# A wait on the eleventh evicted count step ahead of GpSimd's edge-list gathers in a graph layer

## The chip, the cores and the metric

The kernel runs on one core of one Trainium2 chip. The metric is the device time of one execution, in microseconds (us). Before the change three runs took 560.68, 562.6 and 565.33 us; their median is 562.6 us.

## What is computed

```python
msg = node_feat[src] + edge_feat
agg = jax.ops.segment_sum(msg, dst, num_segments=node_feat.shape[0])
h = jax.nn.relu(agg @ W1 + b1)
return h @ W2 + b2
...
h = jnp.maximum(_layernorm(x, axis=-1), 0.0)
x = x + _L0_gnn_ref(h, edge_attr_64, src, dst, ...)
```

There are 6250 nodes with 64 features and 206250 edges, each with a source node, a destination node and 64 features of its own. The edges are sorted by destination, and each node has its own loop among them. All values are float32 and all indices are int32. For every node the kernel adds up the normalized rows of the sources of its edges and the features of the edges, puts the sum through a layer of 128 hidden units, and adds the result to the node's row.

## The kernel before, in words

**Tiles and periods.** The nodes are cut into 49 tiles of 128, and two tiles are taken at a time. So there are 25 periods, j = 0 to 24; LAST = 24 is the short one, with one tile. In a period TensorE does three kinds of work. It counts, for the nodes of period j, how many edges come from each of the 6250 source nodes. It multiplies the counts of the period before, m = j - 1, with the rows of h. And it puts the pair of tiles f = j - 2 through the hidden layer.

**Counting.** A node has at most 64 edges in its list. GpSimd gathers the lists of the two tiles with two indirect DMAs (`gather_slots`, L490 to L500, into `ell`). VectorE marks the slots that belong to the node (`match`, L633 to L645, writing `hi_m`). TensorE turns the list (`turn_codes`, L778 to L785), ScalarE copies it as `codes` (L354). VectorE makes one-hot matrices of its low and high parts, `lo_hot` and `hi_hot` (`hots`, L647 to L663), in four batches of 32 nodes a period. TensorE multiplies them, 16 small matmuls in a count step (`count`, L799 to L813), and there are 16 count steps in a period. Step u fills a buffer of PSUM, and ScalarE evicts it to `counts` (`copy_counts`, L383 to L389). Each eviction adds one to the semaphore `copied`.

**TensorE's order.** Its order within a period is written out in eight parts, v = 0 to 7 (L871 to L915). Each part begins with count steps 2v and 2v + 1. Then come 12 or 13 matmuls with 256 columns: L823, the high sums, in the even parts, and L831, the low sums, in the odd ones. The odd parts go on with matmuls of 24 float32 columns, L845, the edge sums. Part 0 also has the hidden layer, L860, and part 1 its second matmul, L867. Part 3 turns the edges' destinations, L795, and part 4 turns the lists of the next period, L784 and L785.

**VectorE's order.** Each batch of `hots` waits for its codes and for the count step that freed its buffer (L651 to L653). The first batch of period j + 1 so waits for count step 11 of period j, and the second for step 15. After batch 0 and batch 1 comes an edge one-hot, L670; after batch 1 `match(j + 1)` and `add_rows(j - 2)`, L682; after batch 2 `count_below(j + 2)`, L609 and L616; after batch 3 `set_pointers(j + 2)`, L630, which writes `rp_f`, the place in the sorted edges at which the list of each node begins.

**GpSimd's order.** Its loop over j is at L522 to L532. It issues the two row gathers for period j + 1 (`gather_rows`, L469, into `g`), waits for `rp_f` of period j, places the ranges (`place_ranges`, L479, L481 and L485), issues the two list gathers (L496), then makes the edges' relative destinations of period j - 1 (`make_rel`, L507) and adds the bias to rows of x (`add_bias`, L515). GpSimd runs about two periods ahead of TensorE: the lists of period j are gathered while TensorE counts period j - 2. SyncE's queue loads the edge features, two DMAs for each tile, when the buffer of a tile four back has been used.

Of the kernel before, what the change touches and what calls it, by code (L numbers as in the profile page):

```python
# [6 lines left out]
def build_gnn_layer(nc, x, src, dst, edge, w1, b1, w2, b2, out):  # L7
# [14 lines left out]
    LAST = NT // 2  # L22
# [24 lines left out]
    def step_index(j, u):  # L47
        return 16 * j + u
# [25 lines left out]
    with ctx:  # L74
# [6 lines left out]
        def sem(name):  # L81
            return ctx.enter_context(nc.semaphore(name))
# [131 lines left out]
        hots_made, counted, copied = sem("hots_made"), sem("counted"), sem("copied")  # L214
# [13 lines left out]
        with nc.Block() as block:  # L228
# [11 lines left out]
            def _(sp):  # L240
# [44 lines left out]
                for j in range(DTS):  # L285
                    if j < LAST:
                        sp.wait_ge(r0_made, j + 1)
                        _, firsts = nc.values_load_multi_w_load_instructions(
                            r0_i[0:1, 2 * j:2 * j + 2], engines=[mybir.EngineType.SP], min_val=0, max_val=E - RANGE,
                            skip_runtime_bounds_check_because="held to the last range of edges")  # L290
                    else:
                        firsts = [E - RANGE]
                    if j >= 2:
                        sp.wait_ge(rel_made, j - 1)
                    for h in range(tiles_in(j)):
                        load_dst_rows(j, h, firsts[h])
                    if j == 0:
                        load_weights()
                        sp.wait_ge(matched, 1)
                    for h in range(tiles_in(j)):  # L300
                        load_edges(2 * j + h, firsts[h])
                    if j == 2:
                        with nc.allow_non_contiguous_dma(reason="the first dst of each following row"):
                            sp.dma_start(dst_sb[0:ROWP - 1, PER:PER + 1],
                                         dst[PER:E].rearrange("(p e) -> p e", e=PER)[:, 0:1]).then_inc(next_in, 16)
                        sp.dma_start(dst_sb[ROWP - 1:ROWP, PER:PER + 1],
                                     dst[E - 1:E].rearrange("(p e) -> p e", e=1)).then_inc(next_in, 16)
                        sp.wait_ge(h_made, SLICES)
                        sp.dma_start(h_dram.rearrange("(t p) f -> p t f", p=P), h_sb[:, :, :]).then_inc(h_out, 16)
                    if j >= 2:  # L310
                        store_rows(j - 2)
# [106 lines left out]
            def _(pool):  # L418
# [45 lines left out]
                def gather_rows(j):  # L464
                    if j >= 2:
                        pool.wait_ge(below_made, j - 1)
                    for h in range(tiles_in(j)):
                        t = 2 * j + h
                        nc.gpsimd.indirect_dma_start(  # L469
                            out=g2[j % 2][:, h, :], out_offset=None, in_=dst.rearrange("(r e) -> r e", e=STEP),  # L470
                            in_offset=bass.IndirectOffsetOnAxis(ap=row_i[:, t:t + 1], axis=0)).then_inc(rows_in[j % 2], 16)

                def place_ranges(j):
                    n = tiles_in(j)
                    if j >= 2:
                        pool.wait_ge(ell_in[j % 2], 32 * (j // 2))
                    pool.wait_ge(rp_made, j + 1)
                    if j < LAST:
                        nc.gpsimd.tensor_scalar(r0_f[0:1, 2 * j:2 * j + n], rp_f[0:1, 2 * j:2 * j + n],  # L479
                                                float(E - RANGE), None, ALU.min).then_inc(r0_set, 1)  # L480
                    nc.gpsimd.tensor_scalar(ell_idx[j % 2][:, 0:n], rp_f[:, 2 * j:2 * j + n],  # L481
                                            float(E), None, ALU.min).then_inc(idx_made, 1)
                    if j < LAST:
                        pool.wait_ge(r0_set, j + 1)
                        nc.gpsimd.tensor_copy(r0_i[0:1, 2 * j:2 * j + n], r0_f[0:1, 2 * j:2 * j + n]).then_inc(r0_made, 1)  # L485
                    else:
                        pool.wait_ge(shift_made, 1)
                        nc.gpsimd.tensor_copy(ell_idx[j % 2][0:HALF, 1:2], shift_f[0:HALF, :]).then_inc(idx_made, 1)

                def gather_slots(j):  # L490
                    pool.wait_ge(idx_made, j + 1 + (j == LAST))
                    if j >= 2:
                        pool.wait_ge(turned, j - 1)
                    for h in range(2):
                        rows = HALF if j == LAST and h == 1 else P
                        nc.gpsimd.indirect_dma_start(  # L496
                            out=ell[j % 2][0:rows, h, :, :].rearrange("p s w -> p (s w)"), out_offset=None,
                            in_=comb_dram[:, :],
                            in_offset=bass.IndirectOffsetOnAxis(ap=ell_idx[j % 2][0:rows, h:h + 1], axis=0)
                        ).then_inc(ell_in[j % 2], 16)  # L500

                def make_rel(j):
                    n = tiles_in(j)
                    pool.wait_ge(dst_rows_in[j % 2], 32 * (j // 2) + 16 * n)
                    if j >= 2:
                        pool.wait_ge(rel_turned, j - 1)
                    nc.gpsimd.tensor_scalar(rel_rows[j % 2][0:n * CK, :], dst_rows[j % 2][0:n * CK, :],  # L507
                                            float(2 * j * P), tile_base[0:n * CK, 0:1],
                                            ALU.subtract, ALU.subtract).then_inc(rel_made, 1)

                def add_bias(f):
                    tiles = slice(2 * f, 2 * f + tiles_in(f))
                    pool.wait_ge(mean_sub, SLICES)
                    pool.wait_ge(w_in, 80)
                    nc.gpsimd.tensor_tensor(x_sb[:, tiles, :], x_sb[:, tiles, :],  # L515
                                            bc(b2_all[:, :].rearrange("p (o f) -> p o f", o=1), [P, tiles_in(f), F]),
                                            ALU.add).then_inc(bias_added, 1)
# [4 lines left out]
                for j in range(DTS):  # L522
                    if j + 1 < DTS:
                        gather_rows(j + 1)
                    place_ranges(j)
                    if j == 0:
                        pool.wait_ge(comb_out, 48)
                    gather_slots(j)
                    if j >= 1:
                        make_rel(j - 1)  # L530
                    if j >= 2:
                        add_bias(j - 2)  # L532
# [542 lines left out]
```

## Time and profile before

| | |
|---|---|
| median of three runs | 562.6 us (560.68 to 565.33) |
| profiled execution | 561.41 us, span 559.8 us |
| TensorE matmul (PE) | 486.8 us busy, 87% of the span |
| VectorE (DVE) | 428.1 us, 76% |
| ScalarE (ACT) | 355.1 us, 63% |
| GpSimd (POOL) | 268.7 us, 48% |
| mean granted clock of TensorE | 0.988 |

The profile is of one execution; its span is from the first to the last instruction. PE are matmuls, PEld weight loads, which run beside them. A row of the timeline gives the start in us from the beginning of the span, the time in us, the engine, the line of the kernel, the operation with what it writes and reads, and how many instructions are merged in the row. Where the engine sat idle before, the row ends with that idle time and what ended it. "issue" stands for idle time in which the engine waited for nothing that the profile shows.

### The profile page before, as it was taken

The page shows a single profiled execution, that of the slowest core. Times are in us where ns is not written, and L with a number is a line of the kernel's source. Part 1 is how long each engine was busy: PE and PEld are TensorE (multiplying, and loading weights), DVE is VectorE, ACT ScalarE, POOL GpSimd, SP SyncE. Part 2 cuts the span into 40 slices and gives each one's busy share as a digit, 9 for nine tenths or more (in the row PEclk, how much of TensorE's full clock was granted, in tenths as well). Part 3 has the DMA queues.
Part 4 walks back from the last instruction along what each step waited for, and adds up shares of the span by engine and source line. Part 5 has one row for each costly group of instructions (what it writes and reads, how often), then busy time and mean ns, then how long its engine had stood idle before and what let it go on. Part 6 is the DMA issues. An engine that isn't in the chain of part 4 may idle for free.

```text
span 559.8 us, 27476 instructions
## 1 busy us (share of the span) xinstructions
PE 486.8 (87%) x12541; PEld 427.6 (76%) x12541; DVE 428.1 (76%) x456; ACT 355.1 (63%) x503; POOL 268.7 (48%) x249
## 2 busy tenths in 40 slices
PE   1014999999999999999999999999999999998996
PEld 1013788777888888888888888888888888887895
DVE  4999879667887797777787787777788779766941
ACT  3747667665766767656666666666676676575721
POOL 4483774484375366336357347417437535416200
PEclk9999999998999999989999999999999999899999
DMA  9575167453453543633634635435546354354300
GB/s 201 162 216 165 24 200 193 127 167 105 112 176 102 154 141 100 188 102 97 189 105 117 174 101 150 140 99 151 141 110 180 100 154 138 97 152 123 94 7 9
DMA packets 139623, 73.62 MB, mean 132 GB/s; under 512 B 23644, under 2 KB 137550, under 8 KB 139382
## 3 DMA queue, kind: packets, MB, share of 16 engines
q1 hardware_dynamic: 136105, 65.30, 42.4%
q0 software_dynamic: 3168, 4.90, 2.7%
q8 instruction: 99, 1.62, 1.2%
q10 hardware_dynamic: 234, 1.65, 0.9%
q14 instruction: 17, 0.14, 0.1%
HBM read 66.98 MB, written 4.86 MB: 128 GB/s over the span
## 4 chain that ended last, share of the span: by engine, by line
PE 84%; DVE 8%; issue 5%; ACT 1%; DMA 1%; another core or an unknown queue 0%; SPq 0%; DVEq 0%; ACTq 0%
PE sum_ps L823 25%; PE sum_ps L845 20%; PE count_ps L810 18%; PE sum_ps L831 14%; PE head_ps L860 3%; PE head_ps L867 3%; DVE lo_hot L656 2%; PE turn_ps L795 1%; DVE hi_hot L656 1%; DMA dst_sb<-in_dst 1%; DVE h_sb L555 1%; DVE mean L553 1%; DVE h_sb L568 1%; DVE var L561 1%; DVE h_parts L624 1%
## 5 line engine op out<-in xcount | busy, mean ns | idle before, releaser
L387 ACT CAST counts<-count_ps 128x784 bf16<-128x784 f32 x391 | 300.9, 817 | 129.0 <-PE count_ps L810 124.6
L656 DVE TENSOR_TENSOR lo_hot<-iota_lo,codes 128x4096 bf16<-128x4096 bf16 x98 | 224.1, 2286 | 66.8 <-PE count_ps L810 54.4
L823 PE MATMUL sum_ps<-counts,h_parts 128*128 128x256 bf16 (+1 forms) x1225 | 153.8, 277 | 0.0
L845 PE MATMUL sum_ps<-e_hot,edges 128*64 128x24 f32 x3528 | 129.6, 215 | 15.8 <-issue 15.6
L810 PE MATMUL count_ps<-hi_hot,lo_hot 64*128 64x49 bf16 x6256 | 124.9, 184 | 19.1 <-DVE hi_hot L656 11.5
L845 PEld LDWEIGHTS sum_ps<-e_hot,edges 128*64 128x64 f32 x3528 | 124.9, 138 | 20.5 <-issue 19.3
L810 PEld LDWEIGHTS count_ps<-hi_hot,lo_hot 64*128 64x128 bf16 x6256 | 101.5, 95 | 42.8 <-issue 13.4
L823 PEld LDWEIGHTS sum_ps<-counts,h_parts 128*128 128x128 bf16 x1225 | 114.1, 100 | 20.2 <-issue 0.2
L479 POOL TENSOR_SCALAR r_f<-rp_f 1x2 f32<-1x2 f32 x24 | 12.8, 533 | 188.9 <-DVE rp_f L630 188.8
L469 POOL DMA_INDIRECT g<-in_dst,row_i x49 | 88.0, 1796 | 18.3 <-issue 11.5
L656 DVE TENSOR_TENSOR hi_hot<-iota_hi,codes 128x1600 bf16<-128x1600 bf16 x98 | 96.5, 985 | 0.0
L831 PE MATMUL sum_ps<-counts,h_parts 128*64 128x256 bf16 (+1 forms) x1225 | 86.2, 275 | 0.0
L507 POOL TENSOR_SCALAR rel_rows<-dst_rows,tile_base 36x256 f32<-36x256 int32 (+1 forms) x25 | 71.6, 2864 | 4.4 <-DMA dst_rows<-in_dst 2.5
L496 POOL DMA_INDIRECT ell<-comb_rows,ell_idx x50 | 60.4, 1208 | 22.1 <-issue 17.0
L831 PEld LDWEIGHTS sum_ps<-counts,h_parts 128*64 128x64 bf16 x1225 | 59.7, 110 | 5.2 <-issue 0.2
L670 DVE TENSOR_TENSOR e_hot<-win_tab,rel_sb 128x864 f32<-128x864 f32 x49 | 54.8, 1118 | 6.1 <-ACT rel_sb L363 6.1
L372 ACT COPY agg_sb<-sum_ps 128x256 f32<-128x256 f32 (+1 forms) x25 | 9.2, 367 | 27.3 <-issue 11.9
L642 DVE SCALAR_TENSOR_TENSOR hi_m<-ell,node_f 128x64 bf16<-128x64 f32 x50 | 11.9, 278 | 17.4 <-DMA ell<-comb_rows,ell_idx 13.3
L784 PE MATMUL turn_ps<-ident_b,ell 128*128 128x128 bf16 x25 | 5.6, 223 | 21.4 <-DVE hi_m L642 19.0
L682 DVE TENSOR_TENSOR o_sb<-head_ps,x_sb 128x128 f32<-128x128 f32 (+1 forms) x25 | 7.1, 286 | 18.4 <-PE head_ps L867 18.4
L354 ACT COPY codes<-turn_ps 128x512 bf16<-128x512 bf16 x25 | 14.7, 587 | 9.9 <-PE turn_ps L785 9.9
L784 PEld LDWEIGHTS turn_ps<-ident_b,ell 128*128 128x128 bf16 x25 | 2.8, 112 | 21.9 <-issue 21.7
(108 smaller groups left out, 222.3 us busy)
## 6 DMA issues: line engine op xcount, KB each, us to landing
edges<-in_edge_attr SPq DMA_DIRECT2D x98, 576.0 KB
h_rows<-h_sb SPq DMA_DIRECT2D x1, 1568.0 KB, 10.1
x_sb<-in_x SPq DMA_DIRECT2D x4, 384.0 KB, 10.5
out<-o_sb SPq DMA_DIRECT2D x24, 64.0 KB, 3.7
comb_rows<-counts ACTq DMA_DIRECT2D x1, 1443.8 KB
dst_rows<-in_dst SPq DMA_DIRECT2D x49, 18.0 KB
ell<-comb_rows,ell_idx POOLq DMA_INDIRECT x50
g<-in_dst,row_i POOLq DMA_INDIRECT x49
```

What stands on the lines that cost most here:

```text
L387: nc.scalar.copy(counts[j % 2][:, :, 0:2 * half].rearrange("p s (h i) -> p h s i", h=2)[:, :, :, 8 * u:8 * u + 8], count_ps[g % 2][:, :, 0 ...
L469: nc.gpsimd.indirect_dma_start(out=g2[j % 2][:, h, :], out_offset=None, in_=dst.rearrange("(r e) -> r e", e=STEP), in_offset=bass.Indirect ...
L496: nc.gpsimd.indirect_dma_start(out=ell[j % 2][0:rows, h, :, :].rearrange("p s w -> p (s w)"), out_offset=None, in_=comb_dram[:, :], in_off ...
L507: nc.gpsimd.tensor_scalar(rel_rows[j % 2][0:n * CK, :], dst_rows[j % 2][0:n * CK, :], float(2 * j * P), tile_base[0:n * CK, 0:1], ALU.subt ...
L656: return nc.vector.tensor_tensor(out_ap.rearrange("p i (a t) -> p i a t", t=2), bc(table_ap.rearrange("p (o a t) -> p o a t", o=1, t=2), [ ...
L670: nc.vector.tensor_tensor(e_hot[h][:, :, :].rearrange("p (c k) w -> p c k w", k=KK), bc(win_tab[:, m // LAST, :, :].rearrange("p c (o w) - ...
L810: last = nc.tensor.matmul(count_ps[g % 2][:, h, i * NT:(i + 1) * NT], lo_hot[n % 2][rows, at, :], hi_hot[n % 2][rows, at, 0:NT], start=Tru ...
L823: nc.tensor.matmul(sum_ps[m % 2][:, 0:cols], parts[:, s, 0:2 * F], counts[m % 2][:, s, 0:cols], start=(s == 0), stop=False, skip_group_che ...
L831: last = nc.tensor.matmul(sum_ps[m % 2][half, 0:cols], parts[:, s, 2 * F:3 * F], counts[m % 2][:, s, 0:cols], start=False, stop=False, ski ...
L845: last = nc.tensor.matmul(sum_ps[m % 2][half, low:low + W], edges[t % SLOT_EDGES][:, c, k * F:(k + 1) * F], e_hot[h][:, i, :], start=False ...
L860: nc.tensor.matmul(hid_ps[:, 0:cols], w1_sb[:, :], agg_sb[:, 0:cols], start=True, stop=True).then_inc(hid_made, 1)
L867: last = nc.tensor.matmul(out_ps[0:n, h * F:(h + 1) * F], hid_sb[:, h * P:h * P + n], w2_sb[:, :], start=True, stop=True)
```

## The change

GpSimd gets one more wait, behind `place_ranges(j)` and ahead of `gather_slots(j)`, in the loops with j from 2 to 24. It waits until ScalarE has evicted count step 10, the eleventh, of period j - 2. For every j that occurs the expression gives step 10, since j - 2 is below LAST. Nothing else is changed.

```diff
                     place_ranges(j)
                     if j == 0:
                         pool.wait_ge(comb_out, 48)
+                    if 2 <= j:
+                        pool.wait_ge(copied, step_index(j - 2, 10 if j - 2 < LAST else 0) + 1)
                     gather_slots(j)
                     if j >= 1:
                         make_rel(j - 1)
```

## Rows read from the trace of the kernel before

**Rows 1.** The chain of waits that ended last, its shares by engine
```profile
PE 84%; DVE 8%; issue 5%; ACT 1%; DMA 1%; another core or an unknown queue 0%; SPq 0%; DVEq 0%; ACTq 0%
```

**Rows 2.** Waits: who waited for whom, us in total, times, longest
```profile
PE sum_ps L845 <- issue: 15.6, 39, 0.4
...
DVE hi_m L642 <- DMA ell<-comb_rows,ell_idx: 13.3, 4, 4.7
```

**Rows 3.** Timeline of GpSimd over one period
```profile
296.27 0.22 POOL L479 TENSOR_SCALAR r_f<-rp_f 1x2 f32<-1x2 f32 x1 [8.43 <-DVE rp_f L630]
...
297.25 1.00 POOL L496 DMA_INDIRECT ell<-comb_rows,ell_idx  x1 [0.47 <-issue]
298.56 0.94 POOL L496 DMA_INDIRECT ell<-comb_rows,ell_idx  x1 [0.30 <-issue]
299.59 3.19 POOL L507 TENSOR_SCALAR rel_rows<-dst_rows,tile_base 36x256 f32<-36x256 int32 x1
...
303.48 2.91 POOL L469 DMA_INDIRECT g<-in_dst,row_i  x1 [0.16 <-issue]
306.69 1.48 POOL L469 DMA_INDIRECT g<-in_dst,row_i  x1 [0.30 <-issue]
```

**Rows 4.** Timeline of TensorE, the same period and the next one's start
```profile
296.75 0.58 PE L810 MATMUL count_ps<-hi_hot,lo_hot 64*128 64x49 bf16 x32
...
299.30 0.31 PE L845 MATMUL sum_ps<-e_hot,edges 128*64 128x24 f32 x4 [0.40 <-issue]
300.01 0.48 PE L845 MATMUL sum_ps<-e_hot,edges 128*64 128x24 f32 x10 [0.40 <-issue]
...
305.46 0.70 PE L860 MATMUL head_ps<-agg_sb,w_sb 128*128 128x256 f32 x2
...
325.60 0.70 PE L860 MATMUL head_ps<-agg_sb,w_sb 128*128 128x256 f32 x2
```

**Rows 5.** Timeline of VectorE over the same period
```profile
295.95 0.15 DVE L630 TENSOR_TENSOR rp_f<-cnt,row_base 128x2 f32<-128x2 f32 x1
298.64 2.29 DVE L656 TENSOR_TENSOR lo_hot<-iota_lo,codes 128x4096 bf16<-128x4096 bf16 x1 [2.54 <-PE count_ps L810]
...
305.39 0.98 DVE L656 TENSOR_TENSOR hi_hot<-iota_hi,codes 128x1600 bf16<-128x1600 bf16 x1
...
307.26 0.47 DVE L642 SCALAR_TENSOR_TENSOR hi_m<-ell,node_f 128x64 bf16<-128x64 f32 x2
```

**Rows 6.** Timeline of ScalarE, the same stretch
```profile
296.85 0.58 ACT L354 COPY codes<-turn_ps 128x512 bf16<-128x512 bf16 x1 [0.20 <-PE turn_ps L785]
297.34 0.82 ACT L387 CAST counts<-count_ps 128x784 bf16<-128x784 f32 x1
298.57 0.81 ACT L387 CAST counts<-count_ps 128x784 bf16<-128x784 f32 x1 [0.42 <-PE count_ps L810]
```

**Rows 7.** Timeline of GpSimd in an early period
```profile
92.37 2.12 POOL L479 TENSOR_SCALAR r_f<-rp_f 1x2 f32<-1x2 f32 x1 [7.43 <-DVE rp_f L630]
...
96.47 3.04 POOL L496 DMA_INDIRECT ell<-comb_rows,ell_idx  x1 [0.16 <-issue]
99.82 1.51 POOL L496 DMA_INDIRECT ell<-comb_rows,ell_idx  x1 [0.30 <-issue]
```

**Rows 8.** Timeline of VectorE in the same early period
```profile
104.96 0.48 DVE L642 SCALAR_TENSOR_TENSOR hi_m<-ell,node_f 128x64 bf16<-128x64 f32 x2 [4.45 <-DMA ell<-comb_rows,ell_idx]
```

**Rows 9.** Timeline of TensorE, the starts of three early periods
```profile
77.72 0.67 PE L860 MATMUL head_ps<-agg_sb,w_sb 128*128 128x256 f32 x2
...
98.13 0.70 PE L860 MATMUL head_ps<-agg_sb,w_sb 128*128 128x256 f32 x2
...
119.08 0.70 PE L860 MATMUL head_ps<-agg_sb,w_sb 128*128 128x256 f32 x2 [0.27 <-ACT agg_sb L372]
```

**Rows 10.** Timeline of GpSimd, a row gather of 1 us
```profile
242.20 0.96 POOL L469 DMA_INDIRECT g<-in_dst,row_i  x1 [0.30 <-issue]
```

**Rows 11.** Timeline of TensorE behind two such pairs of row gathers
```profile
125.37 0.47 PE L810 MATMUL count_ps<-hi_hot,lo_hot 64*128 64x49 bf16 x22 [0.48 <-issue]
...
243.58 0.89 PE L845 MATMUL sum_ps<-e_hot,edges 128*64 128x24 f32 x23 [0.37 <-issue]
```

## The prediction

> **What bounds the kernel now.** I read the chain of waits first: TensorE holds 84% of it, and "issue" another 5% [rows 1]. So only time in which TensorE stands still counts, and VectorE (76% busy) and GpSimd (48%) matter through what they do to it. The table of waits then says where TensorE stands still without a producer being late: 15.6 us ahead of the edge sums L845, in 39 pieces of at most 0.4 us [rows 2]. The timelines of one period, side by side, show where they lie. GpSimd issues its two list gathers at 297.25 and 298.56, 1.00 and 0.94 us long [rows 3]; TensorE pauses for 0.40 us up to 299.30 and again for 0.40 us up to 300.01, both in the edge sums of part 5 [rows 4]. The same pair stands at the same distance behind the gathers, 1.6 us and 2.4 us after the start of the first, in each of the 18 periods from 133.68 to 480.50. The other three pieces follow row gathers. Those are 36 pieces in 18 periods, 14.7 us of the 15.6 (0.37, 0.33 and 0.21 us are the other three).
>
> The gathers do more than that. Count steps 10 and 11 start at 296.75 and end at 297.33 [rows 4], and the codes are there at 296.85 + 0.58 = 297.43 [rows 6]. Yet ScalarE gets step 11 only at 298.57, after 0.42 us of idleness [rows 6], and VectorE starts the next batch at 298.64, after 2.54 us [rows 5]. Both come 0.3 to 0.4 us after the end of the first gather, 298.25. I take it that a gather holds up TensorE's signals and its supply of instructions for about its last microsecond. The long matmuls L823 and L831 hide such a hold, and a run of short ones, L845 or the count steps, does not. The row gathers of the same period speak for this: they end at 306.39 and 308.17, among L823 and L867, and leave no gap.
>
> **The change, step by step.**
> One: when the wait opens. Step 10 is evicted at 297.34 + 0.82 = 298.16 [rows 6]. With the 0.3 us that GpSimd takes between gathers [rows 3] the first list gather starts at 298.45 in place of 297.25, 1.2 us later. In the first periods the gather is already later than the eviction (96.47, period start 98.13 [rows 7, 9]), and the wait costs nothing.
>
> Two: what the gather then meets. With no gather running, the signal of step 11 comes at once, so VectorE starts `lo_hot` at about 297.55 and ends `hi_hot` 3.19 us later (the same pair is 3.19 from 298.64 on), at 300.74. The first gather falls into it. In the row gathers [rows 3] one that starts beside `lo_hot` takes 2.91 us and ends at 306.39, with `hi_hot`, whose end is 305.39 + 0.98 = 306.37 [rows 5]; the early list gather takes 3.04 us [rows 7]. So the first list gather ends at 300.75, the second runs from 301.05 for 1.5 us [rows 3, 7] to 302.55, 3.05 us later than the present 299.50. On the lock the Trainium skill ("SBUF — State Buffer", "Who interferes with whom") says that a `tensor_tensor` has no 2-port mode and keeps GpSimd only from reading, and infers that it does not stall descriptor generation. By that rule the first gather would not be stretched; the 2.91 us here disagree.
>
> Three: the pauses of TensorE. The gathers' last microseconds now lie at 299.7 to 300.75 and 301.5 to 302.55. Without its pauses TensorE reaches part 6 at about 299.6: first the short count steps, then the high sums for 1.6 us up to some 301.7, then count steps 14 and 15 and the low sums. The first hold lies in long matmuls, the second mostly behind them, much like the row gathers that leave no gap. I take both pauses as gone: 18 periods, -14.7 us. The bounds are 0 (they only move) and -14.7.
>
> Four: what slides behind. GpSimd's queue behind the wait holds the second list gather, L507, L515 and the next two row gathers. VectorE needs the lists at 307.26, or 306.5 with a period shorter by 0.8. In the early period they landed 104.96 - 101.33 = 3.6 us after the second gather's end [rows 7, 8]; 302.55 + 3.6 = 306.2 is still in time, though by only 0.3 us. L507 is read by TensorE a period later, in part 3, and the biased rows later still; SyncE's load of destinations, which waits for L507, has several microseconds. Nothing is paid there. L507 takes 1.2 us, or stands behind the next batch of hots as now (3.19 us [rows 3]); it ends between 303.8 and 306.1. The row gathers then start between 304.4 and 306.7, and the second ends between 306.7 and 309.1. Against a TensorE that is 0.8 us ahead that is 0.7 us earlier to 1.7 us later than the 308.17 of now. They meet less of the hots and become short, and a pause comes back in the edge sums of part 1: 0.37 us behind a short pair [rows 10, 11]. I take it in every period, 18 x 0.37 = +6.7 us; its bounds are 0 and two of 0.48 us in count steps [rows 11], +17.3 us. ScalarE's eviction of steps 13 and 15 may be held too, which is at most 0.2 us a period in the way of step 0; I take 0, since TensorE's even parts have it covered.
>
> The sum, against the profiled execution: 561.4 - 14.7 + 6.7 = 553.4 us. That execution lies 1.2 us under the median, so about 554.5; I say 554.
>
> **The rivals.**
> A, the forecast: pauses gone in part 5, one comes back in part 1. Range 550 to 558. Chance 0.36.
>
> B, nothing comes back, the row gathers staying behind the hots or hidden in L823: 561.4 - 14.7 = 546.7. For it: now they leave no gap. Chance 0.18.
>
> C, the pauses only change their place. Should the gathers not be stretched, they end at 299.45 and 300.7, and the pauses fall into count steps 12 and 13 at 0.48 us each: 561.4 - 14.7 + 17.3 = 564.0. The same time comes out if the row gathers move into the count steps of part 2. This is what the rule cited under Two would give. Against it stands the stretching to `hi_hot`'s end in 303.48 and 96.47 [rows 3, 7]. Here I count too that the wait is mostly open already. Chance 0.22.
>
> D, slower: the pointers come too late. Now `rp_f` is written by 296.10 [rows 5] and GpSimd's L479 runs at 296.27 in 0.22 us [rows 3], before the next `lo_hot`. VectorE is now free to start that at 297.55, so from 1.3 us of delay in `rp_f` on, L479 stands behind it, as in the early period (2.12 us [rows 7]); L481 and L485 do too, the list gathers slide by some 3 us more, the lists land late (VectorE idle for 4.45 us [rows 8]) and so do the next pointers. What can cause it is the second row gather, up to 1.7 us later against TensorE, holding the signal for L682, behind which batches 2 and 3 stand. The periods in that pattern take 98.13 - 77.72 = 20.41 and 119.08 - 98.13 = 20.95 us [rows 9], against 325.60 - 305.46 = 20.14 [rows 4]: +0.54 on the mean, 18 of them +9.7 us, 571 us. For it: the margin is thin. Against it: the early pattern dissolved by itself after a few periods, so a part of the periods is likelier than all. Chance 0.24.
>
> **How the numbers follow.** The likeliest is A, so 554 us. The range goes from B's 546.5 up to 569, near D's end; outside lie D in full and a few mishaps. About 1% (5.6 us) can be told from no change. Faster by more than that: B, nine tenths of A, a little of D's mixed form: 0.51. Within 1%: the rest of A, C nearly whole, a quarter of D: 0.26. Slower: 0.23.
>
> **What would show it.** Step one: a list gather starts 0.3 us after the eviction of step 10. Step two: VectorE's idle ahead of the first batch's `lo_hot` falls from 2.54 to some 1.4 us, and the first gather takes 2.3 us. Step three: the 39 issue pauses of L845 lose 36, the period falls from 20.14 towards 19.4. Step four: new pauses of 0.4 us behind 1 us row gathers; no DMA wait of L642 beyond the early four [rows 2]. D would show as L479 rows of 2.12 us and more idle of L642 before its lists. I am wrong if the gathers start no later than now, or if the pauses do not depend on where the gathers lie.

## The result and the profile after

The changed kernel takes 544.59 us (median of four runs, 542.93 to 546.33), the kernel before 562.28 us (four runs). The ratio is 0.968, interval 0.9625 to 0.9734: 3.2% faster. Ratios and their intervals, here and below, leave out executions more than 1.5% above the fastest of their kernel; medians and ranges keep them. I had said 554 us and a range from 546.5 us. The profiled execution after takes 545.67 us, its span is 543.8 us.

The waits of all engines after, that answer to [rows 2]:

```profile
POOL ell L496 <- ACT counts L387: 29.8, 18, 2.1
...
DVE hi_m L644 <- DMA ell<-comb_rows,ell_idx: 17.6, 5, 4.7
...
PE sum_ps L847 <- issue: 4.8, 11, 0.4
```

The new wait holds GpSimd 18 times, for 1.7 us each on the mean. (Two lines were added, so the edge sums are L847 now and the list match L644.) TensorE's pauses in the edge sums fell from 15.6 us in 39 pieces to 4.8 us in 11. One period of GpSimd, VectorE and TensorE after, to be laid beside [rows 3], [rows 5] and [rows 4]:

```profile
281.33 1.04 POOL L469 DMA_INDIRECT g<-in_dst,row_i  x1 [0.16 <-issue]
282.68 0.96 POOL L469 DMA_INDIRECT g<-in_dst,row_i  x1 [0.31 <-issue]
...
292.76 2.21 POOL L496 DMA_INDIRECT ell<-comb_rows,ell_idx  x1 [1.65 <-ACT counts L387]
295.27 1.51 POOL L496 DMA_INDIRECT ell<-comb_rows,ell_idx  x1 [0.30 <-issue]
296.87 3.39 POOL L507 TENSOR_SCALAR rel_rows<-dst_rows,tile_base 36x256 f32<-36x256 int32 x1
```

```profile
291.80 2.29 DVE L658 TENSOR_TENSOR lo_hot<-iota_lo,codes 128x4096 bf16<-128x4096 bf16 x1 [1.36 <-ACT codes L354]
294.01 0.98 DVE L658 TENSOR_TENSOR hi_hot<-iota_hi,codes 128x1600 bf16<-128x1600 bf16 x1
```

```profile
278.80 0.70 PE L862 MATMUL head_ps<-agg_sb,w_sb 128*128 128x256 f32 x2
...
282.52 1.19 PE L847 MATMUL sum_ps<-e_hot,edges 128*64 128x24 f32 x27
284.15 0.47 PE L847 MATMUL sum_ps<-e_hot,edges 128*64 128x24 f32 x9 [0.44 <-issue]
284.55 0.58 PE L812 MATMUL count_ps<-hi_hot,lo_hot 64*128 64x49 bf16 x32
...
292.27 1.18 PE L847 MATMUL sum_ps<-e_hot,edges 128*64 128x24 f32 x36
293.38 0.58 PE L812 MATMUL count_ps<-hi_hot,lo_hot 64*128 64x49 bf16 x32
...
298.42 0.70 PE L862 MATMUL head_ps<-agg_sb,w_sb 128*128 128x256 f32 x2
```

The first list gather starts behind the codes and step 10, stands behind the hots (2.21 us) and ends at 294.97 with `hi_hot`, at 294.99. VectorE's idle time ahead of that batch fell from 2.54 to 1.36 us. The edge sums of part 5 run through, 1.11 us from their start to the next count step. In part 1 a pause has come back behind the short row gathers. The period shown is 19.62 us in place of 20.14; eleven periods have this pause in part 1, and most of the others take 18.71 us.

Where the prediction missed is in how long a pause is. The same stage in the kernel before, free of gathers in part 1 and with them in part 5:

```profile
288.88 1.18 PE L845 MATMUL sum_ps<-e_hot,edges 128*64 128x24 f32 x36
289.99 0.81 PE L810 MATMUL count_ps<-hi_hot,lo_hot 64*128 64x49 bf16 x32
...
297.94 0.95 PE L845 MATMUL sum_ps<-e_hot,edges 128*64 128x24 f32 x22
...
300.42 0.58 PE L810 MATMUL count_ps<-hi_hot,lo_hot 64*128 64x49 bf16 x32
```

36 edge sums take 1.11 us from their start to the next count step where nothing disturbs them, and 2.48 us in part 5 (2.53 on the mean of the 18 periods with pauses). The two idle pieces of 0.40 us [rows 4] are only a part of the 1.37 us: the matmuls between them and just ahead of them are spread out too, and count as busy. After, the disturbed part 1 takes 2.03 us (2.04 on the mean of 11), 0.92 more than the free one, of which 0.44 shows as idle. The page's groups say the same for the whole execution, before and after (busy us, mean ns of one, idle us before):

```profile
L845 PE MATMUL sum_ps<-e_hot,edges 128*64 128x24 f32 x3528 | 129.6, 215 | 15.8 <-issue 15.6
```

```profile
L847 PE MATMUL sum_ps<-e_hot,edges 128*64 128x24 f32 x3528 | 123.9, 215 | 5.3 <-issue 4.8
```

Busy and idle together are 145.4 us before and 129.2 after, 16.2 us less; the span fell by 16.0. The other differences that I see are smaller and go both ways: the granted clock, 0.988 before and 0.993 after, and 2.2 us of idle time ahead of the high sums, which was not there before.

### The profile page after: what moved, and what is told of

Read it like the earlier page. It is cut to its first block and busy times, and to the rows that moved or that the text cites. A ratio compares the mean times of both kernels' runs of the same rounds, so it can differ in the third digit from the quotient of the medians.

```text
span 543.8 us, 27476 instructions
## 1 busy us (share of the span) xinstructions
PE 479.2 (88%) x12541; PEld 422.3 (78%) x12541; DVE 431.7 (79%) x456; ACT 353.7 (65%) x503; POOL 267.5 (49%) x249
## 3 DMA queue, kind: packets, MB, share of 16 engines
q0 software_dynamic: 3168, 4.90, 3.2%
## 5 line engine op out<-in xcount | busy, mean ns | idle before, releaser
L825 PE MATMUL sum_ps<-counts,h_parts 128*128 128x256 bf16 (+1 forms) x1225 | 151.3, 274 | 2.2 <-issue 2.2
L825 PEld LDWEIGHTS sum_ps<-counts,h_parts 128*128 128x128 bf16 x1225 | 112.4, 99 | 22.2 <-issue 3.4
L847 PE MATMUL sum_ps<-e_hot,edges 128*64 128x24 f32 x3528 | 123.9, 215 | 5.3 <-issue 4.8
L847 PEld LDWEIGHTS sum_ps<-e_hot,edges 128*64 128x64 f32 x3528 | 121.3, 138 | 7.9 <-issue 7.9
L496 POOL DMA_INDIRECT ell<-comb_rows,ell_idx x50 | 93.1, 1862 | 43.9 <-ACT counts L387 29.8
L658 DVE TENSOR_TENSOR hi_hot<-iota_hi,codes 128x1600 bf16<-128x1600 bf16 x98 | 97.6, 996 | 0.0
L833 PE MATMUL sum_ps<-counts,h_parts 128*64 128x256 bf16 (+1 forms) x1225 | 86.3, 276 | 0.0
L507 POOL TENSOR_SCALAR rel_rows<-dst_rows,tile_base 36x256 f32<-36x256 int32 (+1 forms) x25 | 64.9, 2597 | 4.5 <-DMA dst_rows<-in_dst 2.6
L469 POOL DMA_INDIRECT g<-in_dst,row_i x49 | 55.7, 1136 | 18.3 <-issue 11.5
L833 PEld LDWEIGHTS sum_ps<-counts,h_parts 128*64 128x64 bf16 x1225 | 59.8, 110 | 5.3 <-issue 0.2
L644 DVE SCALAR_TENSOR_TENSOR hi_m<-ell,node_f 128x64 bf16<-128x64 f32 x50 | 14.6, 330 | 17.6 <-DMA ell<-comb_rows,ell_idx 17.6
L354 ACT COPY codes<-turn_ps 128x512 bf16<-128x512 bf16 x25 | 14.7, 587 | 12.1 <-PE turn_ps L787 12.1
```

The source lines that it names most:

```text
L354: nc.scalar.copy(codes[j % 2][:, :, :, :], bc(codes_ps.rearrange("p (c i o) -> p c i o", c=2, o=1), [P, 2, P, 2])).then_inc(codes_made, 1)
L469: nc.gpsimd.indirect_dma_start(out=g2[j % 2][:, h, :], out_offset=None, in_=dst.rearrange("(r e) -> r e", e=STEP), in_offset=bass.Indirect ...
L496: nc.gpsimd.indirect_dma_start(out=ell[j % 2][0:rows, h, :, :].rearrange("p s w -> p (s w)"), out_offset=None, in_=comb_dram[:, :], in_off ...
L644: last = nc.vector.scalar_tensor_tensor(out=hi_m[j % 2][:, at], in0=nodes[:, at], scalar=node_f[:, col:col + 1], in1=his[:, at], op0=ALU.n ...
L658: return nc.vector.tensor_tensor(out_ap.rearrange("p i (a t) -> p i a t", t=2), bc(table_ap.rearrange("p (o a t) -> p o a t", o=1, t=2), [ ...
L825: nc.tensor.matmul(sum_ps[m % 2][:, 0:cols], parts[:, s, 0:2 * F], counts[m % 2][:, s, 0:cols], start=(s == 0), stop=False, skip_group_che ...
```

## The experiments

The theory was: a gather holds up TensorE's signals and instruction supply for about its last microsecond, and the change moves that under long matmuls. Rivals: the wait acts in another way; the pauses come from the transfers; any four gathers cost a fixed time; the lists come too late. The kernels ran in groups, each on one chip with the kernel before beside it.

**The wait on another step (e1).**

```diff
-pool.wait_ge(copied, step_index(j - 2, 10 if j - 2 < LAST else 0) + 1)
+pool.wait_ge(copied, step_index(j - 2, 9 if j - 2 < LAST else 0) + 1)
```

> The kernel with the new wait, but on the tenth evicted count step (step 9) instead of the eleventh. In the trace of the kernel before, step 9 is evicted at 296.66 and the first list gather starts at 297.25, so this wait is open when GpSimd comes to it. If the gain comes from where the gathers lie (my theory), nothing moves: the edge sums of part 5 take 2.5 us again in place of 1.12, the period is 20.1 us and the time 560 to 565 us. If the gain came from something else that the wait does (another start of GpSimd's queue, the chip's clock), the time is 543 to 550 us.

546.3 us against 561.17, ratio 0.9735 (0.9673 to 0.9798). I expected nothing and got nearly all of it. GpSimd, VectorE and TensorE:

```profile
289.31 1.00 POOL L496 DMA_INDIRECT ell<-comb_rows,ell_idx  x1 [0.63 <-issue]
290.62 1.86 POOL L496 DMA_INDIRECT ell<-comb_rows,ell_idx  x1 [0.30 <-issue]
```

```profile
289.37 2.29 DVE L658 TENSOR_TENSOR lo_hot<-iota_lo,codes 128x4096 bf16<-128x4096 bf16 x1 [1.36 <-ACT codes L354]
```

```profile
291.42 0.30 PE L847 MATMUL sum_ps<-e_hot,edges 128*64 128x24 f32 x3 [0.44 <-issue]
```

The wait is open, but it is one more instruction: 0.63 us lie ahead of the gather in place of 0.47 [rows 3]. In those 0.16 us the signal of step 11 passes, VectorE starts 0.06 us behind the gather instead of 1.39, and the second gather stands behind the hots. Here the second of the two pauses is gone and the first stays. In every other period VectorE is a little earlier and starts ahead of the gather:

```profile
309.01 2.29 DVE L658 TENSOR_TENSOR lo_hot<-iota_lo,codes 128x4096 bf16<-128x4096 bf16 x1 [1.17 <-ACT codes L354]
309.15 3.04 POOL L496 DMA_INDIRECT ell<-comb_rows,ell_idx  x1 [0.63 <-issue]
```

A gather that starts 0.06 us ahead of `lo_hot` takes 1.00 us, one that starts 0.14 us behind it takes 3.04 us, and then no pause is left. From 297 to 454 us the periods alternate between 18.71 us, with no pause, and 20.57 us, with one pause in part 1 and one in part 5. Over the 17 periods that follow the early pattern of [rows 7 to 9], the settled ones, e1 takes 19.58 us each (140.75 to 473.63) and the changed kernel 19.43 (143.56 to 473.80). So the eviction of step 10 is not needed for nearly all of the gain.

**No list gathers (e2).** From j = 6 on `gather_slots` returns at once, and the waits on its DMAs stop at the last one issued.

```diff
 def gather_slots(j):
+    if j >= 6:
+        return
```

> The kernel before without the list gathers from j = 6 on; the lists of periods 4 and 5 are used again, so the sums are of other edges, with the same instructions on TensorE. If the gathers themselves hold TensorE up, its two pauses in part 5 vanish in these periods, the edge sums there take 1.12 us in place of 2.53, and the period falls from 20.1 to about 18.7 us unless the row gathers come to lie elsewhere (0.9 us if they do): 17 periods less 1.4 us, 24 us, so 535 to 545 us. If the rival holds, that the pauses come from the transfers of edge features (which are unchanged), the period stays 20.1 and the time 560 us or more.

534.12 us, ratio 0.9493 (0.9454 to 0.9532), just under the 535 us I gave. The edge features are loaded as before, the periods are 18.71 us from 276 us on, and the group of the edge sums is 120.2 us busy and 1.6 idle. The gathers cause the pauses, not the transfers of edge features.

**Short lists (e3).** 8 bytes a row from j = 6 on, in as many packets as before (3168 in the gathers' queue in either trace).

```diff
-out=ell[j % 2][0:rows, h, :, :].rearrange("p s w -> p (s w)")
+out=ell[j % 2][0:rows, h, 0, :]
```

> The kernel before with list gathers of 8 bytes a row in place of 512 from j = 6 on; the rest of the lists is left over from earlier periods, so the sums are of other edges. The number of rows and so of descriptors is the same, the bytes moved are a 64th. If it is the making of the descriptors on GpSimd that holds TensorE up, the gathers still take 1.0 us, the pauses stay, the edge sums of part 5 stay at 2.5 us and the time at 558 to 565 us. If it is the data of the gathers beside the edge features, the pauses shrink to little and the time falls to 535 to 545 us.

561.52 us, ratio 1.0026 (0.9988 to 1.0064). GpSimd, and TensorE behind it:

```profile
295.63 1.00 POOL L496 DMA_INDIRECT ell<-comb_rows,ell_idx  x1 [0.47 <-issue]
296.94 0.94 POOL L496 DMA_INDIRECT ell<-comb_rows,ell_idx  x1 [0.30 <-issue]
```

```profile
297.72 0.34 PE L846 MATMUL sum_ps<-e_hot,edges 128*64 128x24 f32 x5 [0.43 <-issue]
298.49 0.53 PE L846 MATMUL sum_ps<-e_hot,edges 128*64 128x24 f32 x10 [0.43 <-issue]
```

The bytes can go and the pauses stay. Nor is it the packets: in the trace of the kernel before, the gathers' queue moves none from 297.25 to 299.89 us, and by then VectorE has started (298.64) and the first pause is over (299.30). What is left is the issuing of the gather on GpSimd.

How the issuing holds the others is not shown, and one place does not fit my theory of the last microsecond. In an undisturbed period of the changed kernel a short row gather starts with the low sums L833, just as the first list gather of the kernel before starts with L831 (297.25 [rows 3] and 297.26), and edge sums follow it too. First the row of the kernel before, then those of the changed one:

```profile
297.26 0.85 PE L831 MATMUL sum_ps<-counts,h_parts 128*64 128x256 bf16 x12
```

```profile
243.52 0.97 POOL L469 DMA_INDIRECT g<-in_dst,row_i  x1 [0.30 <-issue]
```

```profile
243.50 0.85 PE L833 MATMUL sum_ps<-counts,h_parts 128*64 128x256 bf16 x12
244.18 1.18 PE L847 MATMUL sum_ps<-e_hot,edges 128*64 128x24 f32 x36
```

They run through without a pause. In the kernel before the next gather came 0.3 us later, here none does. No run puts a single gather against a pair at one place, so what the long matmuls do, what VectorE's stretching does and what the second gather does was not told apart.

**The relative destinations first (e4).** In the changed kernel:

```diff
 place_ranges(j)
+make_rel(j - 1); add_bias(j - 2)
 pool.wait_ge(copied, ...)
 gather_slots(j)
-make_rel(j - 1); add_bias(j - 2)
```

> The changed kernel with make_rel and add_bias ahead of the new wait and the list gathers, so that they run while GpSimd waits for step 10, and the next row gathers follow the list gathers at once. In the changed kernel a pair of short row gathers in part 1 costs TensorE 0.92 us (its edge sums take 2.04 us in place of 1.12) in about eleven periods. Here the row gathers would start some 0.2 us after the second list gather, stand behind the hots as in the kernel before (about 2.4 us, then 1.5 us) and end in the high sums and the hidden layer of parts 0 and 1. By my theory nothing is then given back: a period of 18.7 us, 533 to 539 us. By the rival that any four gathers cost a fixed time wherever they lie, it stays at 542 to 547 us. If L507 now holds up the first batch of hots, VectorE comes late and it is 550 us or more.

597.49 us against 561.17, ratio 1.0625 (1.0548 to 1.0702). The bias stands behind VectorE's hots, the gathers come later still, and VectorE waits for its lists:

```profile
275.81 2.34 POOL L515 TENSOR_TENSOR x_sb<-x_sb,b_all 128x128 f32<-128x128 f32 x1
278.30 1.61 POOL L496 DMA_INDIRECT ell<-comb_rows,ell_idx  x1 [0.16 <-issue]
280.22 3.02 POOL L496 DMA_INDIRECT ell<-comb_rows,ell_idx  x1 [0.31 <-issue]
...
296.05 2.12 POOL L479 TENSOR_SCALAR r_f<-rp_f 1x2 f32<-1x2 f32 x1 [9.71 <-DVE rp_f L632]
```

```profile
288.40 0.48 DVE L644 SCALAR_TENSOR_TENSOR hi_m<-ell,node_f 128x64 bf16<-128x64 f32 x2 [4.12 <-DMA ell<-comb_rows,ell_idx]
```

This is the early pattern of [rows 7, 8], held for nearly the whole run: my rival D is a real mechanism. Its price is higher than the 9.7 us I gave it, but the 36 us here are not all its own. In every other period four gathers now follow each other into part 1, whose edge sums take up to 3.76 us, and TensorE's granted clock is 0.957, against 0.985 to 0.994 in the kernel before beside it; if TensorE were the limit throughout, that would be up to some 20 us (my estimate: 597.5 x 0.043 less 561.2 x 0.009).

**An always open wait (e5).**

```diff
-pool.wait_ge(copied, step_index(j - 2, 10 if j - 2 < LAST else 0) + 1)
+pool.wait_ge(const_made, 2)
```

> The kernel before with a wait ahead of the list gathers that is always open: on the constants that GpSimd made itself at the start. It says nothing about count steps and only costs GpSimd an instruction. In e1 a wait that should also have been open gave 546.3 us, with the first list gather 0.66 us after the start of count steps 10 and 11 in place of 0.50. Theory: the 0.16 us are enough, since the signal of step 11 then gets through before the gather holds it up, VectorE starts its hots 1.1 us earlier, and the second gather stands behind them. Then this kernel is as e1: 543 to 550 us, the first gather 1.0 us, the second 1.9 us, one pause of some 0.9 us left in part 5. Rival: in e1 it was the count step's semaphore that mattered; then this one is as before, 558 to 564 us.

532.53 us, but the kernel before took 534.35 us in this group: ratio 0.9977 (0.9942 to 1.0011). The chip was another, and the kernel before is 5% faster on it. So this run could not tell what it was made for, and raised a larger question.

**The thirteenth step (e6)** has 12 in place of 10.

> The wait on step 12, the thirteenth, in place of the eleventh: evicted at about 294.5 us where the gather of the changed kernel starts at 292.8, so the first gather comes 2 us later. Theory: the first gather ends at about 296, the second stands behind the next batch of hots (296.1 to 299.3), the lists land 2 to 3 us too late for VectorE and the pattern of the early periods holds for good: L642 waits for its lists in most periods, the row gathers fall in the count steps of part 2; 570 to 600 us. Rival: the later the better, as long as TensorE is in its long matmuls, 535 to 548 us.

560.29 us against 534.35 us, 1.052 (1.047 to 1.057). The pattern is the one I forecast; the time lies under my 570 to 600 us, which were reckoned for a chip with pauses. VectorE waits for its lists in nearly every period:

```profile
DVE hi_m L644 <- DMA ell<-comb_rows,ell_idx: 86.1, 22, 5.4
```

Later is not better. The time from the eleventh step to the lists' deadline has no room for 2 us more.

**The relative destinations in GpSimd's idle time (e7, e13 with the wait, e8 without).**

```diff
 gather_rows(j + 1)
+make_rel(j - 1); add_bias(j - 2)
 place_ranges(j)
 pool.wait_ge(copied, ...)      # not in e8
 gather_slots(j)
-make_rel(j - 1); add_bias(j - 2)
```

> The changed kernel with make_rel and add_bias ahead of place_ranges, in the 7 us in which GpSimd waits for the pointers; the wait on step 10 stays. e4 ran them right ahead of the list gathers and so delayed those. Here the list gathers stay where they are (2.2 and 1.5 us, 1.1 us behind the codes), and the row gathers follow them at once: the first stands behind the second batch of hots, the second ends in parts 0 and 1, as in the kernel before. Theory: neither pair costs TensorE anything, the period is 18.7 us and the time 531 to 537 us. Rival, four gathers cost something wherever they are: 542 to 547 us. Were the lists late, 560 us or more.

> e7 without the wait: the kernel before with make_rel and add_bias ahead of place_ranges and nothing else. The list gathers start 0.50 us after count steps 10 and 11 again and hold up the signal of step 11, as before. Theory: the pauses of part 5 are back, 1.4 us a period, the row gathers cost nothing as before: 557 to 564 us. Rival: the move itself gives the gain, 531 to 545 us.

> make_rel and add_bias ahead of place_ranges with the wait on step 10, as e7, which on a chip without pauses took 549 to 575 us. If what made e7 slow does not depend on the pauses (the first row gather is issued right behind the list gathers and makes the next batch late, or the chain of pointers starts later), it is 550 to 600 us here too, whichever chip it is. If e7 was slow only by the state of its chip, it takes 531 to 540 us.

e7 took 573.01 us (548.71 to 574.99) against 534.35; e8 567.29 us, ratio 1.067 (1.058 to 1.077); e13, on a third chip, 577.25 us against 533.48, 1.076 (1.066 to 1.086). The theory's numbers for e7 and e8 were wrong; what I had given for late lists in e7 (560 us or more) came, and e13 lies in its 550 to 600. The waits of e7; those of e13 are alike, 133.0 and 107.1 us:

```profile
POOL rel_rows L507 <- DMA dst_rows<-in_dst: 130.8, 22, 10.5
DVE hi_m L644 <- DMA ell<-comb_rows,ell_idx: 101.7, 24, 5.6
```

The destinations had not been loaded when GpSimd came to them. It waited 6 us a time, 22 times, at L507, with the pointers' work queued behind it. GpSimd was idle there, but the operands were not.

**The kernel before and the changed one on further chips (e9 to e12, e14).** e11 and e12 are the kernel of e5.

> The kernel before, unchanged, with a profile of its own. In the second group of experiments its runs had a median of 534.35 us, in the first and beside the changed kernel 561 to 562 us; the groups ran on different chips. Theory: the pauses that the gathers cause in part 5 (1.4 us in 18 periods, 25 us) are there on the one and not on the other. If this run takes 530 to 536 us, its edge sums take 1.12 us in every part and the period is 18.7 us; if it takes 558 to 564 us, they take 2.5 us in part 5 as in the first profile. Rival: the second chip is faster all over, then every group of instructions is shorter by 5%.

> The changed kernel, unchanged, beside the kernel before on this chip. Theory: the change is worth what the pauses cost. Where the kernel before takes 558 to 564 us, this takes 542 to 547 us again. Where it takes 530 to 536 us there are no pauses in part 5 to remove, the row gathers cost nothing there either, and this takes 530 to 538 us: no difference above 1%. Rival: the later lists cost something by themselves (they leave VectorE 3 us less), which shows only where the pauses do not: 540 us or more against 534.

> The kernel before with the wait on GpSimd's own constants, open at once, which took 532.5 us beside 534.4 us for the kernel before. Here it shows whether the 0.16 us by which it moves the gathers are enough where the pauses exist: 543 to 550 us by my theory if the kernel before is at 558 to 564 us, as in e1; 558 to 564 us if the eviction's semaphore mattered. If the kernel before is at 530 to 536 us it says nothing, and is 530 to 536 us too.

> The wait on GpSimd's own constants once more. Where the kernel before takes about 561 us: 543 to 550 us if the 0.16 us are enough, 558 to 564 us if the semaphore of the evictions matters. Where the kernel before takes 530 to 536 us, it takes the same, and says nothing on this.

> The changed kernel once more. Where the kernel before takes about 561 us, 542 to 547 us, ratio 0.965 to 0.975. Where it takes 530 to 536 us, the same as it, ratio 0.995 to 1.005.

On one more chip: e9, the kernel before, 533.99 us, and the same kernel's other runs beside it 532.35 us; e10, the changed kernel, 532.6 us, ratio 1.0006 (0.9985 to 1.0027); e11 541.19 us, spread from 532.68 to 558.56. On another: before 533.48, e12 535.49, ratio 1.004 (0.9998 to 1.0082); e14 542.99 us, spread from 535.89 to 560.44; for e11 and e14 there is no ratio. So on the first of these chips the change is worth nothing, as I had said for a chip without pauses; e14 missed my 0.995 to 1.005 and hints at a loss. Its settled periods take 18.71 us, as e9's do, so a loss would lie in the early ones. The profile of e9, GpSimd, ScalarE with VectorE, TensorE and the page's group of the edge sums:

```profile
309.45 1.01 POOL L496 DMA_INDIRECT ell<-comb_rows,ell_idx  x1 [0.47 <-issue]
310.76 2.12 POOL L496 DMA_INDIRECT ell<-comb_rows,ell_idx  x1 [0.30 <-issue]
```

```profile
309.05 0.58 ACT L354 COPY codes<-turn_ps 128x512 bf16<-128x512 bf16 x1 [0.20 <-PE turn_ps L785]
309.77 2.29 DVE L656 TENSOR_TENSOR lo_hot<-iota_lo,codes 128x4096 bf16<-128x4096 bf16 x1 [1.47 <-PE count_ps L810]
```

```profile
310.13 1.18 PE L845 MATMUL sum_ps<-e_hot,edges 128*64 128x24 f32 x36
311.25 0.58 PE L810 MATMUL count_ps<-hi_hot,lo_hot 64*128 64x49 bf16 x32
```

```profile
L845 PE MATMUL sum_ps<-e_hot,edges 128*64 128x24 f32 x3528 | 118.5, 215 | 0.0
```

The same kernel, with the gather at the same place behind count steps 10 and 11. But VectorE starts 0.14 us after its codes are there (309.05 + 0.58 = 309.63) in place of 1.21 us [rows 5, 6]. With the wait, where the gather comes later, it is 0.04 us (291.76 to 291.80), so at most some 0.1 us of this is a hold. TensorE is not held at all: 118.5 us for all edge sums against 145.4. Single instructions are as long as before (2.29, 215 ns); the chip is not faster all over. The executions also differ in how long the early pattern lasts. In the profiled one of e12, with a span of 552.8 us, it lasts for more than half of the periods; in that of e11, the same kernel with a span of 532.1 us, VectorE waits for its lists 3 times and not 15:

```profile
DVE hi_m L644 <- DMA ell<-comb_rows,ell_idx: 63.7, 15, 5.3
```

**Side by side where the pauses exist (e15, e16).** The kernel of e5 and the changed kernel.

> The always open wait. Where the kernel before takes about 561 us: 543 to 550 us if 0.16 us more on GpSimd are enough (theory), 558 to 564 us if the evictions' semaphore matters. Where the kernel before takes 530 to 536 us: the same as it.

> The changed kernel. Where the kernel before takes about 561 us, 542 to 547 us, and 1 to 3 us less than e15. Where it takes 530 to 536 us, 530 to 540 us, the spread coming from how many early periods pass before the lists are in time.

The kernel before took 558.19 us here. e15 took 556.19 us (549.26 to 561.27), ratio 0.986 (0.9756 to 0.9964); e16 took 545.07 us, ratio 0.9754 (0.9652 to 0.9855). e15 met neither of its two forecasts: it gains, but less than e1 did. e16 met its own, but not the 1 to 3 us that I gave between the two; their medians are 11 us apart, and their intervals overlap. Once e15 is in step its gathers look like those of e1, and TensorE's periods alternate between 18.70 and 20.46 us, 19.58 on the mean, like the changed kernel's settled periods with a pause in e16 (19.51 to 19.59):

```profile
405.63 0.70 PE L862 MATMUL head_ps<-agg_sb,w_sb 128*128 128x256 f32 x2
...
426.09 0.70 PE L862 MATMUL head_ps<-agg_sb,w_sb 128*128 128x256 f32 x2
...
444.79 0.70 PE L862 MATMUL head_ps<-agg_sb,w_sb 128*128 128x256 f32 x2
```

But it comes into step only at about 370 us; VectorE waits for its lists 14 times:

```profile
DVE hi_m L644 <- DMA ell<-comb_rows,ell_idx: 61.1, 14, 5.0
```

So in e1 and e15 alike, a wait that is open is enough to put the gathers of a settled period where they cost less. Whether the one on the evictions also shortens the way out of the early pattern is open: in e16's profiled execution, a long one of 555.3 us, the pattern lasted until about 330 us too, and the runs of either kernel differ among themselves by what it takes.

## Why the prediction was wrong

Its direction was right, and in kind so were its steps; the sizes in Three and Four were not. Its time, 554 us, was 9.4 us too high, and 544.59 lies under the range's 546.5.

**One and Two held.** The wait binds in 18 periods, the gather stands behind the hots and ends with them, the second takes 1.5 us. Counted from the start of count steps 10 and 11, I had the first gather start at 1.70 and end at 4.00 us and the second end at 5.80; in the period shown (start 291.08) they do so at 1.68, 3.89 and 5.70. Beside `lo_hot` and `hi_hot`, both `tensor_tensor`, the gather takes 1.2 us more, against the inference in the Trainium skill ("SBUF — State Buffer", "Who interferes with whom") that I cited; the measurement decides.

**Three is the step that failed.** I took the two pieces marked "issue", 0.8 us, for the whole cost: "I take both pauses as gone: 18 periods, -14.7 us". Both are gone, but each pair cost 1.42 us on the mean (2.53 against 1.11; 1.37 in the period shown), because the matmuls around an idle piece are spread out and count as busy. That makes 18 x 1.42 = 25.6 us, 10.9 more than I took. The bound "0 and -14.7" was no bound. For the same reason TensorE without its pauses reaches part 6 at 299.05, not 299.6. The floor was in the trace: the same 36 edge sums in the undisturbed parts.

**Four had the right mechanism, but its size and its count were wrong.** One pause comes back in part 1, 0.93 us on the mean and not 0.37. It came back in 11 periods, not in 18. In five others L507 slips in ahead of the hots (238.52 us, 1.16 us long, with `lo_hot` at 238.67), the row gathers start 1.4 to 1.6 us earlier in the period, and the last microsecond of the second lies under the low sums. I had both cases in the text and took one for all periods. 11 x 0.93 = 10.2 us against my 6.7. With 25.6 removed that is -15.4 us where I had -8.0, and this is 7.4 of the 7.7 us by which the profiled execution (545.67) lies under my 553.4. The edge sums' groups have -16.2 for the whole execution, with smaller disturbances. The count matters as much as the size: with the true sizes and 18 periods the sum would have been 561.4 - 25.6 + 16.7 = 552.5 us, so my two errors of size nearly cancel. Nothing was paid for the lists, which I had put 0.3 us from their deadline: there are 5 waits on them, where the kernel before had 4.

**The rivals.** B had nearly the time (546.7) but not the mechanism, since something did come back; that it came near is luck. C did not happen. D did not either, in this kernel. e6 shows that it is close by, and costs 26 us where it holds nearly throughout; e4 mixes it with new pauses (36 us), and e7, e8 and e13 with the wait at L507 (33 to 44 us).

**What I had no way to see** in one execution: the whole gain hangs on the pauses, and these on the chip. In the first measurement the change gives 3.2%, on the other chip with pauses where it was run 2.5%. On three others no trace has pauses in part 5 as here, the kernel before takes 532 to 534 us, and the change was run on two: a ratio of 1.0006 on one, a hint of a loss on the other. Each chip had one group of runs, so a difference between chips and one between occasions can't be told apart.

## What to carry to other kernels

Where a short stage shows idle pieces that no wait explains, measure the stage from its first instruction to the next stage's, and compare it with the same stage elsewhere in the trace; idle pieces alone gave under 60% of the cost here. An indirect DMA issued from GpSimd can hold up other engines, so look at what runs on TensorE around its end, and try it under long matmuls; but an edit that moves it by 0.16 us may do as much as one that is reasoned out, so run the plain delay beside it. Before a gain of a few per cent is believed, run both kernels on a second chip.

## What the runs showed of the hardware that I had not expected

Issuing a pair of indirect gathers of 128 rows held up other engines in some groups of runs and not in others. In the first measurement and in e3 VectorE's next batch starts 1.4 us behind the first gather's start (297.25 to 298.64, 295.63 to 297.08) and 1.2 to 1.3 us after its codes are there, and 36 small matmuls take 2.5 to 2.6 us in place of 1.11; e15 and e16, on a third occasion, have pauses of the same kind. In e9 the batch starts 0.14 us after its codes and the matmuls take 1.11 us, and in none of the traces of that chip and two others does TensorE stand still in its edge sums. The bytes moved do not matter (512 or 8 a row, 561.17 and 561.52 us). And whether the gather or VectorE's `lo_hot` starts first, by 0.1 us, decides between a gather of 1.00 and one of 3.04 us (e1). What makes the difference between chips was not tried and stays open.
